# Expert tiles of 128 slots, two to a job, with second weights resident and ys groups summed among the last jobs

## The chip, the cores and the metric

The kernel runs on one core of a Trainium2 chip. The metric is the device time of one execution in microseconds. The engines are TensorE (PE in the rows; PEld is its weight loading), VectorE (DVE), ScalarE (ACT), GpSimd (POOL) and SyncE (SP), which here issues most of the DMA transfers. An engine takes its instructions in their written order; semaphores order the engines among each other.

## The reference

A block with two halves. The first is a layer norm, a scan over time that trains a small MLP (a gradient step for every time step) and its application. The second, the only one that the change touches, is a layer norm and a mixture of experts:

```python
logits = jnp.einsum('btd,ed->bte', x, w_router)
probs = jax.nn.softmax(logits, axis=-1)
vals, idx = jax.lax.top_k(probs, TOP_K)                 # TOP_K = 2 of 8 experts
gates = jnp.sum(jax.nn.one_hot(idx, N_EXPERTS, dtype=x.dtype) * vals[..., None], axis=-2)
hs = jax.nn.gelu(jnp.einsum('btd,fd->btf', x, Ws1) + bs1)   # shared expert
acc = jnp.einsum('btf,df->btd', hs, Ws2) + bs2
h = jax.nn.gelu(jnp.einsum('btd,efd->btef', x, W1) + b1)
y = jnp.einsum('btef,edf->bted', h, W2) + b2
acc = acc + jnp.einsum('bted,bte->btd', y, gates)
return SCALE * acc
```

There are 4 x 1024 tokens of 128 features, the hidden width is 512, all is float32. Only the two chosen experts of a token are computed.

## The kernel before

Up to about 352 us the program does the first half. Then 4096 tokens in 8 groups (NG) of 4 chunks of 128 are normalised and routed. Every token is written twice into the DRAM buffer xs by GpSimd (dispatch, an indirect transfer of 128 rows): each expert has a region there, and the slots in it are filled in the order of the tokens.

The work behind that is a list of jobs, JOBS. An expert job takes a tile of 256 consecutive slots of one expert (39 tiles, since the fill of each expert is known only at run time: 8192 slots and a partly filled tile for each expert). A shared job takes 256 tokens through the shared expert; nine of its 16 tiles are done before the list begins, five stand between the first expert tiles and two at the end. The first N_FULL = 9 tiles are full ones from the first half of the tokens, so they can run while GpSimd still dispatches the second half.

Which expert and which rows a tile has is computed on VectorE into the tables e_i and row_i (full_tiles for the first nine, other_tiles for the rest, the latter between post(6) and post(7) ahead of the list). For each tile SyncE reads these with value_load and issues two transfers: rows(j), 256 rows of xs into xt, and weights(j), the expert's two weight matrices and biases into slab, a ring of RW = 5 buffers. weights(j) waits until VectorE has added tile j-5's bias (e_yb), rows(j) until tile j-4 has been turned (e_tx). The program order of SyncE is: weights of the first five tiles, then for each tile rows(j), weights(j); weights of tiles 9 and 10 come ahead of the rows of tile 9, which need the end of the dispatch.

On TensorE a loop over the list does this for job i:

```python
for i in range(len(JOBS)):
    feed_for(i + 2)
    if i + 1 < len(JOBS):
        e_up(i + 1)
    e_down(i)
```

feed turns the rows of a tile (two 128x128 transposes), VectorE copies them to hg (e_high), e_up makes four 128x256 products with the first weights, ScalarE applies the gelu (e_gelu, one activation for each product), and e_down makes eight 128x128 products with the second weights. VectorE adds the bias and scales the rows with their gates (e_post); its order for job i is prepare(i + 2), which is e_high and meta, then e_post(i). GpSimd scatters the 256 result rows to ys in DRAM, at twice the token's index plus 0 or 1 (scatter, two indirect transfers a tile); rows that belong to no token of this expert go to dump rows.

When all scatters have landed (all_scattered), SyncE loads ys in eight groups into yg, TensorE adds the two results of each token with two products by the identity, VectorE multiplies by the gate, adds to xr, and SyncE and ScalarE store the groups to the output. In the trace a float32 product shows as two MATMUL instructions with two weight loads.

## Time and profile before

| | us |
|---|---|
| median of 3 runs (lowest, highest) | 633.46 (633.27, 637.78) |
| the profiled execution, its own time | 635.85 |
| its span, first to last instruction | 634.1 |
| TensorE matmuls busy | 576.8 (91%) |
| VectorE busy | 427.3 (67%) |
| GpSimd busy | 389.8 (61%) |
| ScalarE busy | 333.7 (53%) |

The span is what the trace covers; the execution's own time is 1.75 us longer. Times of the trace count from the first instruction. Busy time of TensorE is that of overlapping, pipelined instructions; how long a piece of work really takes is read from the starts of consecutive ones.

### The profile page before, as it was taken

The numbers are of one execution on the slowest core, as the hardware profiler recorded it, in microseconds if no ns is written. First come the engines' busy times: TensorE is split into PE (matmuls) and PEld (weight loads), VectorE is DVE, ScalarE is ACT, GpSimd is POOL, SyncE is SP. The second block draws the span as 40 slices with busy tenths as digits, with TensorE's granted clock in tenths as the row PEclk, the third lists the DMA queues.
The fourth block names the chain that finished last, engine by engine and source line by source line (L and its number), as shares of the span: only waits on it lengthen the run. The fifth ranks groups of instructions, "written<-read, shape, count | busy, mean of one in ns | idle before, by whom it ended". The sixth has DMA issues, their size and how long they took to land. (4 is left out here: it accounts for less than half of the span.)

```text
span 634.1 us, 14457 instructions
## 1 busy us (share of the span) xinstructions
PE 576.8 (91%) x4324; PEld 512.9 (81%) x4324; DVE 427.3 (67%) x1730; ACT 333.7 (53%) x1064; POOL 389.8 (61%) x598
## 2 busy tenths in 40 slices
PE   2469999999999999999996967899999999999976
PEld 2249999899999999999984566788999999999952
DVE  3736888788788888878885579876553455545426
ACT  2455666566666656666662374894444444444410
POOL 1526666656666665666662607888888888887520
PEclk9999999999999999999998869899999999999989
DMA  9069930000000000000000001163564778777357
GB/s 196 6 260 394 395 150 1 2 0 0 0 0 0 0 0 0 0 0 0 2 2 1 2 0 39 45 231 95 156 186 130 216 244 247 230 235 232 103 201 212
DMA packets 39797, 66.77 MB, mean 105 GB/s; under 512 B 7523, under 2 KB 26725, under 8 KB 39749
## 3 DMA queue, kind: packets, MB, share of 16 engines
q1 hardware_dynamic: 31076, 54.85, 27.5%
q0 software_dynamic: 4544, 9.45, 4.2%
q10 hardware_dynamic: 4128, 1.91, 1.4%
q8 instruction: 22, 0.36, 0.2%
q14 instruction: 27, 0.21, 0.1%
HBM read 36.26 MB, written 29.92 MB: 104 GB/s over the span
## 5 line engine op out<-in xcount | busy, mean ns | idle before, releaser
L1575 ACT ACTIVATE hid<-bank,slab 128x256 f32<-128x256 f32 x156 | 64.2, 471 | 80.6 <-PE bank L1428 80.5
L1987 POOL DMA_INDIRECT ys<-yo,dst x78 | 75.2, 964 | 28.9 <-issue 16.6
L1979 POOL DMA_INDIRECT xs<-hrow,slot_i x64 | 62.7, 979 | 35.4 <-issue 35.4
L1442 PEld LDWEIGHTS bank<-slab,hid 128*128 128x128 f32 x624 | 75.8, 192 | 2.0
L1442 PE MATMUL bank<-slab,hid 128*128 128x128 f32 x624 | 76.0, 275 | 0.0
L1428 PE MATMUL bank<-hg,slab 128*128 128x256 f32 x312 | 73.7, 380 | 0.4 <-DVE hg L1842 0.4
L1875 DVE TENSOR_TENSOR yb<-bank,slab 128x256 f32<-128x256 f32 x39 | 16.6, 425 | 74.1 <-PE bank L1442 74.1
L1428 PEld LDWEIGHTS bank<-hg,slab 128*128 128x128 f32 x312 | 56.3, 190 | 6.7 <-issue 0.6
L986 POOL TENSOR_TENSOR nL<-aL,ones 128x128 f32<-128x128 bf16 x32 | 16.9, 528 | 41.4 <-ACT aL L695 41.4
L409 PE MATMUL bank<-aH,W2p 128*128 128x128 f32 x192 | 42.1, 301 | 0.1
L409 PE MATMUL bank<-kv,W1b 128*128 128x128 f32 x192 | 41.4, 298 | 0.0
L998 POOL TENSOR_TENSOR nH<-aH,ones 128x128 f32<-128x128 f32 x32 | 14.6, 457 | 36.7 <-ACT aH L713 36.7
L1962 POOL MEMSET rested<- 128x1408 f32 x25 | 32.3, 1291 | 0.0
L409 PEld LDWEIGHTS bank<-aH,W2p 128*128 128x128 f32 x192 | 28.9, 190 | 3.3 <-DVE W2p L790 0.3
L409 PE MATMUL bank<-GX,ge 128*128 128x128 f32 x128 | 30.7, 322 | 0.6 <-DVE ge L790 0.5
L409 PEld LDWEIGHTS bank<-kv,W1b 128*128 128x128 f32 x192 | 29.8, 196 | 0.1
L990 POOL TENSOR_TENSOR oL<-tL,ones 128x128 f32<-128x128 f32 x32 | 14.6, 456 | 24.7 <-ACT tL L698 24.7
L1880 DVE TENSOR_SCALAR yo<-yb,gt 128x128 f32<-128x128 f32 x78 | 26.5, 471 | 1.4
L1013 POOL TENSOR_TENSOR diff<-ge 128x256 f32<-128x256 f32 x32 | 23.3, 728 | 5.5 <-DVE sums L793 5.5
L790 DVE SCALAR_TENSOR_TENSOR gL<-qrowL,bank 128x128 bf16<-128x128 bf16 x64 | 18.4, 287 | 11.1 <-ACT qrowL L706 5.5
L970 POOL TENSOR_TENSOR GXb<-GX,ones 128x256 bf16<-128x256 f32 x32 | 23.3, 729 | 4.0 <-DVE GX L790 2.1
L409 PE MATMUL bank<-hT,wkv 128*128 (+1 forms) x128 | 23.3, 307 | 2.5 <-POOL arowL L1033 2.5
(340 smaller groups left out, 1872.3 us busy)
## 6 DMA issues: line engine op xcount, KB each, us to landing
slab<-in_slabs_dram SPq DMA_DIRECT2D x39, 578.0 KB, 4.2
xs<-fill SPq DMA_DIRECT2D x34, 528.0 KB
xt<-xs SPq DMA_DIRECT2D x39, 132.0 KB
yg<-ys SPq DMA_DIRECT2D x8, 512.0 KB, 6.7
xr<-in_L_attn_x_dram SPq DMA_DIRECT2D x16, 128.0 KB, 6.9
ys<-yo,dst POOLq DMA_INDIRECT x78, 3.8
xs<-hrow,slot_i POOLq DMA_INDIRECT x64, 2.5
out_dram<-xr SPq DMA_DIRECT2D x16, 64.0 KB, 1.8
```

What stands on the lines that cost most here:

```text
L409: return pe.matmul(dst, lhs, rhs, start=start, stop=stop, skip_group_check=True)
L790: return dve.scalar_tensor_tensor(out=dst, in0=a, scalar=s, in1=b, op0=o0, op1=o1)
L970: pool.tensor_tensor(GXb[r][:, :, :].rearrange("p k t -> p (k t)"), GX[r][:, :, :].rearrange("p k t -> p (k t)"), ones2[:, :], ALU.mult).t ...
L986: pool.tensor_tensor(nL[1][:, :], aL[1][:, :], ones2[:, 0:P], ALU.subtract).then_inc(l_n, 1)
L1013: pool.tensor_tensor(diff[:, :, :], ge[r % 2][1][:, :, :], ge[r % 2][0][:, :, :], ALU.subtract).then_inc(chk_d, 1)
L1428: mm = pe.matmul(e_half(i, n), left[:, n * P:(n + 1) * P], right, start=True, stop=True)
L1442: mm = pe.matmul(y[:, s * D:(s + 1) * D], hid[i % 2][:, n, s * P:(s + 1) * P], right, start=(n == 0), stop=(n == FT - 1), skip_group_check ...
L1575: nc.scalar.activation(hid[i % 2][:, n, :], e_half(i, n), ACT.Gelu_apprx_tanh, bias=bias).then_inc(e_x, 1)
L1880: dve.tensor_scalar(yo[v][:, s, :], yb[i % 2][:, s, :], gt[v][:, s:s + 1], None, ALU.mult).then_inc(e_yo, 1)
L1962: nc.gpsimd.memset(rested[:, :], 0.0).then_inc(pause_done, 1)
L1979: pool.indirect_dma_start(out=xs[:, :], out_offset=bass.IndirectOffsetOnAxis(ap=slot_i[:, i, c:c + 1], axis=0), in_=hrow[:, c, :], in_offs ...
L1987: pool.indirect_dma_start(out=ys[:, :], out_offset=bass.IndirectOffsetOnAxis(ap=dst[v][:, s:s + 1], axis=0), in_=yo[v][:, s, :], in_offset ...
```

## The change

- A tile is 128 slots (HALF), and an expert job takes two of them, which may belong to different experts. There are 72 half tiles, so 36 expert jobs in place of 39; 12 of them (N_FULL) come before the end of the dispatch, in place of 9.
- SyncE reads an expert and a row for each half: two rows transfers of 128 rows and two slab transfers a job. A slab now holds the first weights and the biases only; the ring has RW = 4 buffers of two slabs.
- The second weights of all experts are loaded once into w2 (2 MB). e_down on TensorE reads the experts of its two halves from e_i and picks the weights by register.
- e_up makes eight products of 128 columns; e_gelu eight activations.
- The tiles behind the first twelve are listed in three parts: by the end of the first half, of the third quarter and of all of the dispatch. The tables for them are computed in four pieces on VectorE behind jobs 1 to 4. So after BY_HALF (20) jobs' tiles the first four groups of ys are complete, after BY_THREE (28) two more.
- SyncE loads groups 0 to 3 of ys after the weights of tiles 30 to 33, groups 4 and 5 behind the last tile, 6 and 7 when all scatters have landed. VectorE adds the two results itself for groups 0 to 6 (group_step, three operations a group, among the posts of jobs 34 to 42 and behind them); TensorE does it for group 7.

```diff
-SLAB = 2 * F + FT + D
-N_TILES = (2 * B * S) // TS + E - 1
+SLAB = F + FT + D
+HALF = P
+N_HALVES = -(-((2 * B * S) // HALF + E - 1) // SUB) * SUB
+N_TILES = N_HALVES // SUB
 CAP = B * S
 N_SH = B * S // SH
 PARTS = ((0, 2), (2, 4), (4, 6), (6, 8))
 LONGEST = 8
-N_FULL = -(-(B * S - E * (TS - 1)) // TS)
+N_FULL = -(-(B * S - E * (HALF - 1)) // HALF) // SUB
+FULL = N_FULL * SUB
...
+BY_HALF = -(-((B * S + E * (HALF - 1)) // HALF) * HALF // TS)
+BY_THREE = -(-((3 * B * S // 2 + E * (HALF - 1)) // HALF) * HALF // TS)
...
+LOAD_AT = N_TILES - 6
+ADD_AT = len(JOBS) - (N_SH - EARLY_SH - 5) - 7
 RX = 4
 RY = 10
-RW = 5
+RW = 4
...
-            slab = [psb(f"slab{i}", [P, SLAB]) for i in range(RW)]
+            slab = [psb(f"slab{i}", [P, SUB, SLAB]) for i in range(RW)]
+            w2 = psb("w2", [P, E, F])
             hg = [psb(f"hg{i}", [P, TS]) for i in range(2)]
-            hid = [psb(f"hid{i}", [P, FT, TS]) for i in range(2)]
+            hid = hs
...
-                    e = sp.value_load(e_i[0:1, j:j + 1], min_val=0, max_val=E - 1)
-                    sp.dma_start(slab[j % RW][:, :], slabs[:, bass.ds(e, 1), :].rearrange("p o w -> p (o w)")).then_inc(s_slab[j % RW], 16)
+                    for s in range(SUB):
+                        e = sp.value_load(e_i[0:1, SUB * j + s:SUB * j + s + 1], min_val=0, max_val=E - 1)
+                        sp.dma_start(slab[j % RW][:, s, :], slabs[:, bass.ds(e, 1), :].rearrange("p o w -> p (o w)")).then_inc(s_slab[j % RW], 16)
 
                 def rows(j):
                     if j >= RX:
                         sp.wait_ge(e_tx, j - RX + 1)
                         sp.wait_ge(meta_ready, j - RX + 1)
-                    row = sp.value_load(row_i[0:1, j:j + 1], min_val=0, max_val=XS_ROWS - TS)
-                    sp.dma_start(xt[j % RX][:, :, :], xs[bass.ds(row, TS), :].rearrange("(s p) w -> p s w", p=P)).then_inc(s_xt[j % RX], 16)
-
+                    for s in range(SUB):
+                        row = sp.value_load(row_i[0:1, SUB * j + s:SUB * j + s + 1], min_val=0, max_val=XS_ROWS - HALF)
+                        sp.dma_start(xt[j % RX][:, s, :], xs[bass.ds(row, HALF), :]).then_inc(s_xt[j % RX], 16)
+
+                sp.dma_start(w2[:, :, :], e_w2).then_inc(s_w2, 16)
...
-                all_scattered(sp)
-                for g in range(NG):
-                    load(sp, g)
-                for g in range(0, NG, 2):
-                    store(sp, g)
+                    if j == LOAD_AT:
+                        scattered(sp, BY_HALF)
+                    if LOAD_AT <= j < LOAD_AT + 4:
+                        load(sp, j - LOAD_AT)
+                scattered(sp, BY_THREE)
+                load(sp, 4)
+                load(sp, 5)
+                store(sp, 0)
+                store(sp, 2)
+                scattered(sp, N_TILES)
+                load(sp, 6)
+                load(sp, 7)
+                store(sp, 4)
+                store(sp, 6)
...
-                        mm = pe.matmul(e_half(i, n), left[:, n * P:(n + 1) * P], right, start=True, stop=True)
+                        if kind == "expert":
+                            for s in range(SUB):
+                                mm = pe.matmul(e_half(i, n)[:, s * P:(s + 1) * P], slab[j % RW][:, s, n * P:(n + 1) * P],
+                                               hg[j % 2][:, s * P:(s + 1) * P], start=True, stop=True)
+                        else:
+                            mm = pe.matmul(e_half(i, n), left[:, n * P:(n + 1) * P], right, start=True, stop=True)
...
+                    if kind == "expert":
+                        if j == 0:
+                            pe.wait_ge(s_w2, 16)
+                            pe.wait_ge(table_ready, 2)
+                        if j == N_FULL:
+                            pe.wait_ge(table_ready, 4)
+                        expert = [pe.value_load(e_i[0:1, SUB * j + s:SUB * j + s + 1], min_val=0, max_val=E - 1) for s in range(SUB)]
                     if i >= 2:
                         pe.wait_ge(e_yb, i - 1)
                     for s in range(SUB):
                         for n in range(FT):
                             if s == 0:
                                 pe.wait_ge(e_x, FT * i + n + 1)
-                            right = slab[j % RW][:, F + n * P:F + (n + 1) * P] if kind == "expert" else sw[:, 1, n, :]
+                            right = w2[:, bass.ds(expert[s], 1), n * P:(n + 1) * P].rearrange("p o w -> p (o w)") if kind == "expert" else sw[:, 1, n, :]
...
-                for g in range(NG):
-                    pe.wait_ge(s_yg[g], 16)
-                    if g >= 2:
-                        pe.wait_ge(sum_used, g - 1)
-                    for k in range(2):
-                        mm = pe.matmul(bank[6 + g % 2][:, :], ident[:, :], yg[g][:, :, k * D:(k + 1) * D], start=(k == 0), stop=(k == 1))
-                    mm.then_inc(sum_ready, 1)
+                pe.wait_ge(s_yg[NG - 1], 16)
+                for k in range(2):
+                    mm = pe.matmul(bank[7][:, :], ident[:, :], yg[NG - 1][:, :, k * D:(k + 1) * D], start=(k == 0), stop=(k == 1))
+                mm.then_inc(sum_ready, 1)
...
+                        if kind == "expert":
+                            nc.scalar.activation(hid[i % 2][:, n, 0:P], e_half(i, n)[:, 0:P], ACT.Gelu_apprx_tanh,
+                                                 bias=slab[j % RW][:, 0, F + n:F + n + 1])
+                            nc.scalar.activation(hid[i % 2][:, n, P:TS], e_half(i, n)[:, P:TS], ACT.Gelu_apprx_tanh,
+                                                 bias=slab[j % RW][:, 1, F + n:F + n + 1]).then_inc(e_x, 1)
...
+                def rest_marks():
+                    grid = [P, V, CAP // HALF]
+                    dve.wait_ge(turned, NG)
+                    then(dve.tensor_tensor(over_all, held[:, :, :].rearrange("p k e -> p (k e)").unsqueeze(2).broadcast_to(grid),
+                                           cut["step"].unsqueeze(1).broadcast_to(grid), ALU.is_gt))
+                    then(dve.tensor_reduce(marks[:, E:4 * E], over_all, AX_X, ALU.add))
...
+                def rest_ends():
+                    then(dve.tensor_tensor(number[:, :], marks[:, E:4 * E], marks[:, 0:3 * E], ALU.subtract))
...
+                    for k in range(3):
+                        then(dve.tensor_tensor(tri[:, k * E:(k + 1) * E, :], number[:, k * E:(k + 1) * E].unsqueeze(1).broadcast_to([P, E, E]),
+                                               cut["tri"].rearrange("p (a b) -> p a b", b=E), ALU.mult))
+                    then(dve.tensor_reduce(last[:, :, :].rearrange("p k e -> p (k e)"), tri[:, :, :], AX_X, ALU.add))
+                    for k in range(1, 3):
+                        then(dve.tensor_scalar(last[:, k, :], last[:, k, :], last[:, k - 1, E - 1:E], None, ALU.add))
+
+                def rest_experts():
+                    then(dve.tensor_tensor(later, cut["tile"][:, 0:n_rest].unsqueeze(2).broadcast_to([P, n_rest, V]),
+                                           last[:, :, :].rearrange("p k e -> p (k e)").unsqueeze(1).broadcast_to([P, n_rest, V]), ALU.is_ge))
+                    then(dve.tensor_reduce(etab[:, rest], later, AX_X, ALU.add))
+                    for k in range(1, 3):
+                        then(dve.scalar_tensor_tensor(out=etab[:, rest], in0=later[:, :, k * E - 1], scalar=-float(E), in1=etab[:, rest],
+                                                      op0=ALU.mult, op1=ALU.add))
+                    dve.tensor_scalar(e_i[:, rest], etab[:, rest], float(E - 1), None, ALU.min).then_inc(table_ready, 1)
+
+                def rest_rows():
...
+                    then(dve.tensor_tensor(later, later, weight[:, :].unsqueeze(1).broadcast_to([P, n_rest, V]), ALU.mult))
+                    then(dve.tensor_reduce(first[:, rest], later, AX_X, ALU.add))
...
+                    dve.tensor_copy(row_i[:, rest], rowf[:, rest]).then_inc(table_ready, 1)
+
+                def group_step(k):
+                    g = k // 3
+                    y, xc = ysum[g % 2][:, :, :], xr[:, g * GRP:(g + 1) * GRP, :]
+                    if k % 3 == 0:
+                        dve.wait_ge(s_yg[g], 16)
+                        dve.tensor_tensor(y, yg[g][:, :, 0:D], yg[g][:, :, D:2 * D], ALU.add).then_inc(sum_used, 1)
+                    elif k % 3 == 1:
+                        dve.wait_ge(sum_used, 2 * g + 1)
+                        dve.tensor_tensor(y, y, gate[:, 1, :].unsqueeze(1).broadcast_to([P, GRP, D]), ALU.mult).then_inc(sum_used, 1)
+                    else:
+                        dve.wait_ge(sum_used, 2 * g + 2)
+                        dve.wait_ge(sh_ready, min(N_SH, (g + 1) * GRP // SUB))
+                        dve.tensor_tensor(xc, y, xc, ALU.add).then_inc(fin_ready, 1)
...
+                    if i == 1:
+                        rest_marks()
+                    elif i == 2:
+                        rest_ends()
+                    elif i == 3:
+                        rest_experts()
+                    elif i == 4:
+                        rest_rows()
+                    elif ADD_AT <= i < ADD_AT + 4:
+                        group_step(2 * (i - ADD_AT))
+                        group_step(2 * (i - ADD_AT) + 1)
+                    elif ADD_AT + 4 <= i < ADD_AT + 7:
+                        group_step(i - ADD_AT + 4)
+                        if i == ADD_AT + 6:
+                            group_step(11)
+                            group_step(12)
+                    elif i == ADD_AT + 7:
+                        group_step(13)
+                for k in range(14, 18):
+                    group_step(k)
```

How this stands in the instruction streams. SyncE, before: one tile of the steady state, its rows and the next weights. ISA rows are register operations and the check of the value's bounds.

```order
L1295 TENSOR_LOAD row_i [waits h_e,h_W1]
L1295 ISA x2
L1296 ISA
L1296 DMA xt0<-xs 128x2x132
L1288 TENSOR_LOAD e_i [waits h_T2]
L1288 ISA x2
L1289 ISA
L1289 DMA slab3<-in_slabs_dram 128x1156
```

SyncE now, at the same place: the two rows transfers of a tile and the first of its two slab transfers.

```order
L1306 TENSOR_LOAD row_i [waits h_e,h_W1]
L1306 ISA x2
L1307 ISA
L1307 DMA xt0<-xs 128x132
L1306 TENSOR_LOAD row_i
L1306 ISA x2
L1307 ISA
L1307 DMA xt0<-xs 128x132
L1298 TENSOR_LOAD e_i [waits h_T2]
L1298 ISA x2
L1299 ISA
L1299 DMA slab0<-in_slabs_dram 128x644
```

A tile has four groups of a table read, register operations and an issue, in place of two; only the first of each pair carries waits.

TensorE, before: e_up of a tile (L1428) and e_down of the one before it (L1442).

```order
L1428 MATMUL bank2<-hg0,slab0 128x256 [waits h_Tq,h_U2,h_n]
L1428 MATMUL bank2<-hg0,slab0 128x256
L1428 MATMUL bank3<-hg0,slab0 128x256 x2
L1442 MATMUL bank4<-slab4,hid0 128x128 [waits h_Tq,h_T2]
L1442 MATMUL bank4<-slab4,hid0 128x128 [waits h_Tq] x3
L1442 MATMUL bank4<-slab4,hid0 128x128 x4
```

TensorE now: the last products of e_up (L1450), then the start of e_down (L1466, L1474).

```order
L1450 MATMUL bank2<-hg0,slab2 128x128 x3
L1450 MATMUL bank3<-hg0,slab2 128x128 x4
L1466 TENSOR_LOAD e_i
L1466 ISA x2
L1466 TENSOR_LOAD e_i
L1466 ISA x2
L1474 ISA [waits h_Tq,h_T2]
L1474 MATMUL bank4<-w2,hs0 128x128
L1474 ISA [waits h_Tq]
L1474 MATMUL bank4<-w2,hs0 128x128
L1474 ISA [waits h_Tq]
```

Two table reads stand ahead of the first down product, and a register operation, which carries the wait for the gelu, ahead of each.

VectorE now, behind the post of job 3 (rest_experts) and up to the copy of the next tile's columns (L1907); before, nothing stood between a post and that copy.

```order
L1868 TENSOR_SCALAR last<-last 128x8 [waits et_step] x2
L1939 TENSOR_TENSOR yb1<-bank5,slab2 128x256 [waits h_Ta,et_step]
L1944 TENSOR_SCALAR yo2<-yb1,gt2 128x128 [waits h_e,h_T2]
L1944 TENSOR_SCALAR yo2<-yb1,gt2 128x128
L1871 TENSOR_TENSOR xn<-tabs,last 128x1152
L1873 TENSOR_REDUCE etab<-xn 128x48 [waits et_step]
L1875 SCALAR_TENSOR_TENSOR etab<-xn,etab 128x48 [waits et_step] x2
L1877 TENSOR_SCALAR e_i<-etab 128x48 [waits et_step]
L1907 COPY hg0<-bank6 128x256 [waits h_U1,h_W1]
L1913 TENSOR_TENSOR other<-xt0,etab 128x2
```

These operations have moved from ahead of the list into it.

## Rows read from the trace of the kernel before

**Rows 1.** Windows by stage, core 0: busy time (instructions) of each engine, clock, DMA

```profile
438.00:490.00 52.00, 51.19 (x347) 47.83 (x348) 24.27 (x86) 23.08 (x56) 42.81 (x43) 1.00 0.51 147
490.00:598.00 108.00, 108.00 (x754) 102.02 (x753) 55.18 (x231) 47.65 (x116) 84.90 (x83) 1.00 0.74 224
```

**Rows 2.** The chain of waits from 430 to 500: start, duration, what

```profile
482.80 2.24 DMA xt<-xs
...
485.53 1.73 PE bank L1428 x8
487.26 1.78 PE bank L1442 x16
```

**Rows 3.** Timeline of TensorE, 438 to 484: start, us, instructions merged

```profile
439.24 3.69 PE L1428 MATMUL bank<-hg,slab 128*128 128x256 f32 x16 [0.39 <-DVE hg L1842]
...
455.52 0.38 PE L1410 MATMUL bank<-ident,xt 128*128 128x128 f32 x2
...
459.26 0.38 PE L1410 MATMUL bank<-ident,xt 128*128 128x128 f32 x2
...
481.21 1.89 PE L1428 MATMUL bank<-hg,slab 128*128 128x256 f32 x8
```

**Rows 4.** Timeline of SyncE's transfer issues, 426 to 634

```profile
433.43 8.57 SPq L1296 DMA_DIRECT2D xt<-xs  x6
...
486.36 0.34 SPq L1289 DMA_DIRECT2D slab<-in_slabs_dram  x1
487.53 0.37 SPq L1296 DMA_DIRECT2D xt<-xs  x1
...
491.01 0.35 SPq L1289 DMA_DIRECT2D slab<-in_slabs_dram  x1
```

**Rows 5.** The instructions of line 1288 on SyncE: ns min/median/max

```profile
L1288 SPq TENSOR_LOAD <-e_i x39: 262/273/448, 415.0 to 586.6; - x39
L1288 SPq FUSED_REGOPS  x39: 147/147/154, 415.3 to 586.9; - x39
L1288 SPq SEQ_ASSERT  x39: 18/18/18, 415.5 to 587.1; - x39
```

**Rows 6.** The page's list of transfers: KB each, us from issue to landing

```profile
slab<-in_slabs_dram SPq DMA_DIRECT2D x39, 578.0 KB, 4.2
...
xt<-xs SPq DMA_DIRECT2D x39, 132.0 KB
```

**Rows 7.** Timelines of all engines and of VectorE: start, us, instruction, idle before

```profile
432.32 0.40 DVE L1798 TENSOR_REDUCE etab<-past 128x30 f32<-128x240 f32 x1
...
434.47 0.24 DVE L1807 TENSOR_SCALAR rowf<-rowf,taken 128x30 f32<-128x30 f32 x1
...
478.54 0.42 DVE L1842 COPY hg<-bank 128x256 f32<-128x256 f32 x1
...
616.12 0.69 DVE L1947 TENSOR_TENSOR ysum<-bank,gate 128x512 f32<-128x512 f32 x1 [5.61 <-PE bank L1520]
```

**Rows 8.** The chain of waits from 598, then a row of TensorE's timeline

```profile
602.50 1.80 PE bank L1442 x16
...
605.83 0.96 POOL ys L1987
...
607.09 2.24 DMA ys<-yo,dst
...
609.47 3.81 DMA yg<-ys
...
613.33 15.71 PE bank L1520 x32
...
629.79 0.69 DVE xr L1951
...
614.96 0.34 PEld L1520 LDWEIGHTS bank<-yg,ident 128*128 128x128 f32 x1 [0.47 <-DMA yg<-ys]
```

158 lines of the change are left out of this document (75 added, 83 removed).

## The prediction

> **What bounds the kernel now.** The change touches only the last third of the program, so I read the profile in this order. The windows by stage show what TensorE does there: it is busy for 51.19 of 52 us between 438 and 490, and for all of 108 us between 490 and 598, at full granted clock [rows 1]. VectorE, ScalarE and GpSimd are busy for 51%, 44% and 79% of the second window. The chain of waits agrees: from 485.53 it is nothing but TensorE's up and down matmuls, 1.73 and 1.78 us a job [rows 2]. The timeline of TensorE gives the pitch: 455.52 to 459.26, 3.74 us for an expert job (0.22 of them for turning a tile's rows), 3.51 for a shared one [rows 2, 3]. Behind the jobs comes a tail in one chain: the last expert matmul ends at 604.30, the last rows of ys have landed at 609.33, the first group of them is back at 613.28, TensorE sums eight groups for 15.71 us, VectorE ends at 630.48 and the output at 634.1 [rows 8]. So 46 jobs bound 165 us, then 30 us are a serial tail.
>
> The engine to look at next is SyncE. It reads each tile's expert and row from a table before it can issue the transfer. With all waits over, four such steps take 486.36 to 491.01, 1.16 us each, with two more issues between the rows shown [rows 4]; in a step the table read is 0.27 us, its register operations 0.15, the issue itself 0.35 [rows 4, 5]. Two steps a tile, 2.3 us, now hide under 3.74.
>
> **The change part by part.** Times below are in the trace of before, whose span is 634.1.
>
> Fewer jobs. Tiles go from 39 to 36, jobs from 46 to 43. Tensor work of an expert job: the four up products on 256 columns become eight on 128, 16 instructions in place of 8. The down product already has that shape, 16 instructions in 1.78 us [rows 2], so up costs 1.78 in place of 1.73, and a loop is 3.78. Taken by TensorE alone: 3 x 3.74 saved, 36 x 0.05 lost, 9.4 us gained.
>
> SyncE. Each tile now needs two rows transfers and two slab transfers, four steps of 1.16, which is 4.64 us, more than TensorE's 3.78. Halving the bytes does not halve a step: slab transfers of 578 KB and rows transfers of 132 KB are both issued at that pitch [rows 4, 6]. The bounds for a step are 1.0 (if the second of a pair, which has no waits, saved all that lies between the shown parts) and 1.2; I take 1.16. Where five shared jobs lie between the first twelve tiles this is covered. For the 24 tiles behind them nothing covers it, and SyncE becomes what the jobs wait for.
>
> TensorE's own table reads. The second weights are resident, so e_down reads two experts into registers and computes an address before each of eight products. By SyncE's rows a read with its checks is 0.27 + 0.15 + 0.02 [rows 5], up to 0.8 with the gaps, so 0.9 to 1.6 us a job, and up to 0.15 for each of the eight address operations. Whether this costs anything depends on how far TensorE's instruction stream runs ahead of its array, which this trace doesn't show. What it must be ahead by is worked out so: the address operations wait for the gelu results. A gelu of 128 columns costs less than 0.47 us and the eight overlap, so they end some 3.8 us after the job's up began, against 5.5 us for the start of its down. The stream has 1.7 us of lead there, and between two such points it must fit the reads into 3.78. I take it as hidden (cost 0), with 1.6 us a job as the other end. The Trainium skill's page "TensorE: Matmul & The Clock Gate" (section on the array's architecture) gives TensorE an instruction queue 64 deep, which would hold most of a job's 72 weight loads and matmuls, and speaks for hiding; no run here shows it. The page "DMA: Bandwidth & Descriptors" (Latency and other measured facts) puts the floor of a table read at about 600 ns; the trace has 273 ns, and by the page's figure, an estimate, a SyncE step would be 1.5 us and the 24 tiles' stage 31 us longer.
>
> VectorE. The tables of the later tiles move from ahead of the jobs (they were hidden there: TensorE was still at work) into jobs 1 to 4, and grow. An operation on 240 elements takes 0.40 and on 512 0.69 [rows 7], 1.07 ns an element, so 768 elements take 0.97 and 1152 take 1.37; small ones 0.24. rest_marks is 2 x 0.97 = 2.0, rest_ends about 2.2, rest_experts 2 x 1.37 + 3 small = 3.4, rest_rows 2 x 1.37 + 4 small = 3.8. Between the copy of hg (ends 478.96) and the up that reads it (481.21) there are 2.25 us [rows 3, 7]. Playing the four jobs through with VectorE's own 1.8 us a job, the copies for jobs 6 and 7 come 0.9 and 2.1 us late: 3.0 us lost, bounds 0 and 5. Later, 18 summing operations of 0.69, two a job, fit into the slack of 4.64 us jobs.
>
> The tail. Four groups of ys are loaded during the last tiles, two more behind them, and VectorE adds six (and then the seventh) itself. After the last ys rows have landed only two loads, one sum on TensorE and one group on VectorE are left, in place of 8 loads and 32 matmuls.
>
> ScalarE does eight gelus in place of four; it is at 44% [rows 1] and stays under 80% of a loop. GpSimd issues 72 scatters in place of 78 at an unchanged pitch; it was not late at 598 and has more time a tile now. The DMA engines carry 12% more bytes per tile (slabs of 660 KB in place of 578) but fewer tiles, over longer jobs. These cost 0.
>
> **The sum.** Rows transfers start at 433.43 [rows 4]. The fourth of them (tile 1's second half) starts 3 x 1.16 later and lands in 2.24 [rows 2]: up(0) begins at 439.4 (439.24 before [rows 3]). To the end of down of job 13 TensorE has 15 ups, 14 downs and 10 turns: 11 x 1.78 + 4 x 1.73 + 14 x 1.78 + 10 x 0.22 = 53.6, so 493.0, with VectorE's delay 496.0. Job 13 is tile 9; when VectorE has added its bias (0.45 later, 496.45) its slab buffer is free, and since SyncE waits there in order ahead of tile 12's rows, everything else starts from this point. Up to the last rows transfer, that of tile 35, SyncE has 2 + 48 + 42 = 92 steps: 106.7 us; four loads of yg at 0.5 are put among them: 605.2. The rows land at 607.0. Then 0.22 for the turn and three more loops (down of tile 35 comes two jobs after its turn): 10.6, at 617.9, against 602.5 to 604.3 for tile 38's in the old kernel. From there to the landed ys rows 5.03 as before [rows 8]: 622.9. Two loads: the first took 3.81, the second of before was there by 614.96, 5.5 after [rows 8]; with only two in flight I take 4.9 and 0.1 for the issue: 627.95. TensorE's sum to VectorE's start 2.79 (613.33 to 616.12 [rows 7, 8]), two operations 1.42, output 3.62: 635.8.
>
> That is a span 1.7 us longer: the tail falls from 29.8 us after the last expert matmul to 17.9, and this and the three jobs pay for SyncE's pace. The profiled execution took 635.85 us for its span of 634.1, and 637.5 would be the same for the new kernel; the median of the runs lies 2.4 lower, at 633.46, so I predict 635.2. About 1% (6 us) is what a measurement of this kernel can tell from no change.
>
> **Rivals.** (A) The forecast: SyncE paces the later tiles, 629 to 642 with the bounds of step, VectorE's delay and loads. A hundredth of a us in the step is 0.9 us in the end. Chance 0.53, mostly within 1%, with its upper edge beyond.
>
> (B) Slower: TensorE's table reads are not hidden. At 1.6 us a job a loop is 5.4. Twelve tiles of the first stage add 19 us, and the 24 others, bounded by TensorE now and not by SyncE, 24 x 0.74 = 18: 672. It begins to cost in the first stage as soon as the instruction stream needs over 3.78 us a job (at 4.3, 6 us in all: 641), and everywhere over 4.64. For it speaks that the address operations carry the waits, so the stream stops at each gelu; against it the 1.7 us of lead. Chance 0.25.
>
> (C) Faster: SyncE doesn't bind, because steps without waits overlap better than the rows of before show. It decides at 0.95 us a step; then TensorE paces all jobs, down of tile 35 ends at about 601 in place of 617.9 and the time is 618. Against it: the pitch of 1.16 holds wherever steps follow each other. Chance 0.12.
>
> (D) The change doesn't do what it says at the tail: VectorE stands in front of a group that hasn't landed, with the jobs' posts behind it, or the last loads are held up. Up to half of the 12 us gained there goes: 641. The first load is issued some 9 us ahead of its use, which speaks against it. Chance 0.10.
>
> **How the numbers follow.** Faster by over 1%: C and a corner of A, 0.15. Slower by over 1%: B, half of D and the upper edge of A, 0.38. The rest 0.47. For eight in ten the range reaches up into B and down to half of the way to C: 624 to 658.
>
> **What would show it.** In the new trace SyncE's steps should follow without a pause from about 497 to 605 at 4.64 a tile, TensorE should idle 0.8 us a tile on rows just landed, and be without a pause in the first stage but for jobs 5 and 6, where VectorE's copy is late. Idle time ahead of the down products, put down to nothing or to TensorE's own sequencer, would be B. A tile pitch of 3.8 late in the program would be C. I would be wrong in size if reading SyncE's table slows down while TensorE reads it too.

## The result and the profile after

The changed kernel took 651.8 us (median of 4 runs, 647.6 to 656.8). The kernel before, on the same chip at the same time, took 635.6 (4 runs, 633.3 to 640.3). The ratio is 1.023, with an interval of 1.017 to 1.029: slower by 2.3%. The forecast was 635.2 with a range of 624 to 658, so the time lies in the range, and on the side that had a chance of 0.38, 16.6 us above the forecast itself. The profiled execution has a span of 650.0 us against 634.1, at a mean granted clock of 0.961 against 0.976.

The windows by stage of the changed kernel (columns as in [rows 1]):

```profile
438.00:500.00 62.00, 56.07 (x429) 53.91 (x428) 37.37 (x121) 28.00 (x93) 51.43 (x49) 0.94 0.53 150
500.00:560.00 60.00, 53.68 (x453) 52.20 (x453) 23.35 (x114) 29.64 (x108) 37.26 (x37) 0.97 0.64 186
560.00:630.00 70.00, 59.82 (x505) 57.57 (x505) 33.27 (x136) 32.04 (x116) 38.53 (x38) 1.00 0.77 229
```

TensorE, which was busy in 159 of 160 us of this part before [rows 1], is now busy in 169.6 of 192, and its clock is below full in the first two windows. What it waits for is in the view of waits (443 to 629 us: engine, line, releaser, us in total, times, longest):

```profile
PE bank L1431 <- DMA xt<-xs: 16.4, 13, 3.5
PE bank L1450 <- issue: 4.8, 2, 3.3
```

16.4 us go to rows that have not landed when a tile's turn comes (L1431), 4.8 us to two waits ahead of up products (L1450). Those two are where VectorE has tables to build. TensorE's timeline (start, us, instructions merged, idle before and its end), to be laid beside [rows 3]:

```profile
443.91 3.81 PE L1450 MATMUL bank<-hg,slab 128*128 128x128 f32 x32 [0.39 <-DVE hg L1907]
...
466.08 2.02 PE L1450 MATMUL bank<-hg,slab 128*128 128x128 f32 x16 [1.53 <-issue]
467.94 1.95 PE L1474 MATMUL bank<-sw,hs 128*128 128x128 f32 x16
473.18 3.76 PE L1450 MATMUL bank<-hg,slab 128*128 128x128 f32 x16 [3.29 <-issue]
476.73 3.19 PE L1474 MATMUL bank<-w,hs 128*128 x16
479.75 0.38 PE L1431 MATMUL bank<-ident,xt 128*128 128x128 f32 x2
...
505.95 1.95 PE L1450 MATMUL bank<-hg,slab 128*128 128x128 f32 x16
507.74 1.95 PE L1474 MATMUL bank<-w,hs 128*128 x16
513.17 0.47 PE L1431 MATMUL bank<-ident,xt 128*128 128x128 f32 x2 [3.48 <-DMA xt<-xs]
513.45 3.58 PE L1453 MATMUL bank<-hT,sw 128*128 128x256 f32 x8
```

And VectorE at the second of the two waits, with the GpSimd operation beside it (two timelines, the second a single row):

```profile
467.50 1.34 DVE L1880 TENSOR_TENSOR xn<-xn,weight 128x1152 f32<-128x1152 f32 x1
468.88 1.35 DVE L1881 TENSOR_REDUCE first<-xn 128x48 f32<-128x1152 f32 x1
470.26 0.21 DVE L1882 TENSOR_TENSOR rowf<-tabs,first 128x48 f32<-128x48 f32 x1
470.51 1.78 DVE L1883 TENSOR_SCALAR rowf<-rowf,marks 128x48 f32<-128x48 f32 x1
472.32 0.21 DVE L1884 SCALAR_TENSOR_TENSOR rowf<-etab,rowf 128x48 f32<-128x48 f32 x1
472.56 0.19 DVE L1887 CAST row_i<-rowf 128x48 int32<-128x48 f32 x1
472.66 0.42 DVE L1907 COPY hg<-bank 128x256 f32<-128x256 f32 x1
```

```profile
470.96 1.27 POOL L2055 TENSOR_TENSOR xr<-xr,gsb 128x512 f32<-128x512 f32 x1
```

The copy of hg, for which the up at 473.18 waits, stands in order behind rest_rows. rest_rows takes 5.16 us (467.50 to 472.66), of which 1.78 is an operation on 48 elements that takes 0.2 elsewhere in the same list; it ends when GpSimd's operation does (472.29 and 472.23). When TensorE comes back, its next 16 products take 3.76 us and then 3.19 in place of 1.95. The granted clock is 0.91 from 470 to 473 us, 0.50 (the lower of its two levels) from 473 to 476.5, 0.60 from there to 480 and 1.00 again behind it. The same happens at 513.45, where eight products take 3.58 in place of 1.89 (granted clock 0.57 from 513 to 517).

From there on SyncE sets the pace. Its timeline of issues, in the steady part and at its end (compare [rows 4]):

```profile
516.71 1.43 SPq L1299 DMA_DIRECT2D slab<-in_slabs_dram  x2
518.96 1.42 SPq L1307 DMA_DIRECT2D xt<-xs  x2
521.14 1.43 SPq L1299 DMA_DIRECT2D slab<-in_slabs_dram  x2
523.40 1.42 SPq L1307 DMA_DIRECT2D xt<-xs  x2
...
612.34 1.46 SPq L1299 DMA_DIRECT2D slab<-in_slabs_dram  x2
614.62 1.42 SPq L1307 DMA_DIRECT2D xt<-xs  x2
```

Pair follows pair at 2.2 us, 4.43 us for the four steps of a tile (516.71 to 521.14), where TensorE needs 3.78. Over thirteen tiles (527.67 to 586.68) the mean is 4.54, since single steps take a few tenths longer now and then. The end, in the chain of waits (compare [rows 8]; the last expert product ends at 628.96):

```profile
630.67 0.96 POOL ys L2074
631.62 0.30 POOLq L1200
631.93 3.47 DMA ys<-yo,dst
635.72 0.34 SPq L1278
636.11 5.09 DMA yg<-ys
641.24 3.79 PE bank L1549 x4
645.06 0.70 DVE ysum L2034
645.78 0.69 DVE xr L2038
```

21.0 us from the last expert product to the end, where it was 29.8.

### The profile page after: what moved, and what is told of

Its sections match the earlier page's. It is cut to its first block and busy times, and to the rows that moved or that the text cites. A ratio compares the mean times of both kernels' runs of the same rounds, so it can differ in the third digit from the quotient of the medians.

```text
span 650.0 us, 15857 instructions
## 1 busy us (share of the span) xinstructions
PE 567.3 (87%) x4506; PEld 513.9 (79%) x4506; DVE 436.8 (67%) x1755; ACT 347.8 (54%) x1196; POOL 383.9 (59%) x591
## 3 DMA queue, kind: packets, MB, share of 16 engines
q10 hardware_dynamic: 4128, 1.91, 1.3%
## 5 line engine op out<-in xcount | busy, mean ns | idle before, releaser
L2074 POOL DMA_INDIRECT ys<-yo,dst x72 | 69.5, 966 | 58.1 <-DVE yo L1944 46.0
L1604 ACT ACTIVATE hs<-bank,slab 128x128 f32<-128x128 f32 x144 | 54.9, 381 | 83.5 <-PE bank L1450 83.5
L2066 POOL DMA_INDIRECT xs<-hrow,slot_i x64 | 64.3, 1004 | 35.5 <-issue 35.2
L1450 PE MATMUL bank<-hg,slab 128*128 128x128 f32 x576 | 72.0, 280 | 5.2 <-issue 4.8
L1450 PEld LDWEIGHTS bank<-hg,slab 128*128 128x128 f32 x576 | 68.7, 196 | 5.8 <-issue 5.8
L1474 PE MATMUL bank<-w,hs 128*128 x576 | 71.5, 278 | 0.0
L1474 PEld LDWEIGHTS bank<-w,hs 128*128 128x128 f32 x576 | 69.2, 195 | 0.5
L1939 DVE TENSOR_TENSOR yb<-bank,slab 128x256 f32<-128x256 f32 x36 | 15.3, 424 | 76.8 <-PE bank L1474 76.8
L1606 ACT ACTIVATE hs<-bank,slab 128x128 f32<-128x128 f32 x144 | 55.5, 386 | 0.0
L2049 POOL MEMSET rested<- 128x1408 f32 x24 | 30.9, 1289 | 0.0
L416 PEld LDWEIGHTS bank<-kv,W1b 128*128 128x128 f32 x192 | 29.8, 196 | 0.1
L1431 PE MATMUL bank<-ident,xt 128*128 128x128 f32 x72 | 14.5, 285 | 17.2 <-DMA xt<-xs 16.4
```

Of the source, the lines that this page charges most:

```text
L416: return pe.matmul(dst, lhs, rhs, start=start, stop=stop, skip_group_check=True)
L1431: tr = pe.transpose(fed(j)[:, s * P:(s + 1) * P], xt[j % RX][:, s, 0:D], ident[:, :])
L1450: mm = pe.matmul(e_half(i, n)[:, s * P:(s + 1) * P], slab[j % RW][:, s, n * P:(n + 1) * P], hg[j % 2][:, s * P:(s + 1) * P], start=True, s ...
L1474: mm = pe.matmul(y[:, s * D:(s + 1) * D], hid[i % 2][:, n, s * P:(s + 1) * P], right, start=(n == 0), stop=(n == FT - 1), skip_group_check ...
L1604: nc.scalar.activation(hid[i % 2][:, n, 0:P], e_half(i, n)[:, 0:P], ACT.Gelu_apprx_tanh, bias=slab[j % RW][:, 0, F + n:F + n + 1])
L1606: nc.scalar.activation(hid[i % 2][:, n, P:TS], e_half(i, n)[:, P:TS], ACT.Gelu_apprx_tanh, bias=slab[j % RW][:, 1, F + n:F + n + 1]).then_ ...
```

## The experiments

They are numbered e1 to e12 in the order below (e1 is the first, with one more table read). They ran in three groups of four, each group on one chip with the kernel before beside it. Which chip the result came from is not on record; its time for the kernel before (635.6) and its trace are like those of the first group. The kernel before took 634.4 us on the first chip, 642.8 on the second, 643.3 on the third, so only ratios are compared between groups. A second figure is used where a profiled run began its jobs early or late: the time from up(0), the first product of the job list, to the end of the span. It is 206.1 us in the changed kernel (443.91 to 650.0). Three theories were on trial. SyncE: its four steps a tile pace the jobs behind the dispatch. VectorE: the tables hold up the first jobs. TensorE's table reads (the rival B): they cost time ahead of each down product.

**One more table read in each slab step.** On SyncE, in weights:

```diff
                     for s in range(SUB):
                         e = sp.value_load(e_i[0:1, SUB * j + s:SUB * j + s + 1], min_val=0, max_val=E - 1)
+                        e = sp.value_load(e_i[0:1, SUB * j + s:SUB * j + s + 1], min_val=0, max_val=E - 1)
```

> The changed kernel, but SyncE reads the expert of each half tile twice: two more table reads with their checks for a tile, by the trace 0.27 + 0.15 + 0.02 us each, about 0.5 with gaps. If SyncE paces the 24 tiles behind the dispatch, the time grows by 24 x 1.0 us = 24 (to some 675 against 651.8), since every step of its stream counts. If TensorE's own table reads pace the jobs, SyncE has 0.3 us a tile to spare and more, and the time grows by 17 or less; if TensorE's matmuls paced them (3.78 a loop against 4.43 for SyncE now, 5.4 then) the growth would be 24 as well, but from a lower level that the trace of the changed kernel excludes.

Measured: ratio 1.055 (1.047 to 1.064), 673.2 us, span 670.1. That is 3.2 points more than the changed kernel, 20 us for 48 more reads with their register operations behind the dispatch. This profiled run began its jobs at 439.15 us, 4.8 earlier than the changed kernel's; from up(0) on it takes 231.0 us in place of 206.1, 24.9 more, as the expectation has it. That is 0.52 for each read, where one alone is 0.27 + 0.15 and gaps [rows 5]. A step on SyncE is on the path with its full price.

**No table reads on TensorE.** The second weights of fixed experts are used, so that e_down reads no table and computes no address; the rows of the expert tiles are then other numbers than the reference's, with the same work.

```diff
-                        expert = [pe.value_load(e_i[0:1, SUB * j + s:SUB * j + s + 1], min_val=0, max_val=E - 1) for s in range(SUB)]
+                        expert = [(SUB * j + s) % E for s in range(SUB)]
```

> The changed kernel without the table reads and address operations on TensorE: the second weights are those of a fixed expert (the results of the expert tiles are not the reference's). If TensorE's stream runs far enough ahead, as the trace of the changed kernel suggests (no idle time ahead of the down products outside jobs 4 to 6), nothing changes: 652 within 5. If the reads cost their 0.9 to 1.6 us a job, 30 to 50 us go.

Measured: 650.2 us, ratio 1.018 (1.008 to 1.027), and a span of 650.0, to the tenth that of the changed kernel. Rival B is out. The changed kernel's trace shows what was hidden (line 1466, TensorE's sequencer, ns min/median/max):

```profile
L1466 PEldq TENSOR_LOAD <-e_i x72: 296/301/710, 445.7 to 625.2; - x72
L1466 PEldq FUSED_REGOPS  x72: 146/151/156, 446.1 to 625.7; - x72
```

0.45 us a read, 0.9 a job, and no idle time of TensorE before a down product (L1474) in that trace.

**Shorter steps on SyncE.** One table read brings both values of a pair, and the check of their bounds is left out (the table's values keep them):

```diff
-                    for s in range(SUB):
-                        e = sp.value_load(e_i[0:1, SUB * j + s:SUB * j + s + 1], min_val=0, max_val=E - 1)
+                    _, both = nc.values_load_multi_w_load_instructions(
+                        e_i[0:1, SUB * j:SUB * (j + 1)], engines=[mybir.EngineType.SP], min_val=0, max_val=E - 1, ...)
+                    for s in range(SUB):
+                        e = both[s]
```

and the same for the rows.

> The changed kernel with cheaper SyncE steps: one table read fetches both values of a pair, and the bounds checks are left out (the tables are clamped). By the durations in the trace a tile's four steps, 4.43 us now, lose 2 x 0.35 for reads and 4 x 0.2 for checks: 2.9 us, below TensorE's 3.78. If SyncE paces the late tiles, 24 x 0.65 = 16 us go: 636. If it does not, nothing goes.

Measured: 636.4 us, ratio 1.001 (0.996 to 1.006), span 631.8. SyncE's timeline in that kernel:

```profile
544.25 0.85 SPq L1302 DMA_DIRECT2D slab<-in_slabs_dram  x2
545.85 0.85 SPq L1313 DMA_DIRECT2D xt<-xs  x2
547.95 0.89 SPq L1302 DMA_DIRECT2D slab<-in_slabs_dram  x2
```

Pair follows pair at 1.6 us (544.25 to 545.85) in place of 2.2, so SyncE now waits for the others: a tile takes 3.79 us on average (521.54 to 567.05, twelve tiles), which is TensorE's own pace. TensorE's waits for rows fall from 16.4 to 7.0 us. The ratio gives back all 2.3 points, but not all of that is SyncE: in the profiled run the jobs also began at 439.19 in place of 443.91 us. From up(0) to the end it takes 192.6 us, 13.5 less than the changed kernel. With the first experiment, this shows SyncE's pace from both sides. Reading both values at once and leaving out the bounds check were not tried apart.

**Tables spread over nine jobs.** The four functions are cut in nine and one piece is put behind each of jobs 1 to 9.

```diff
-                    if i == 1:
-                        rest_marks()
-                    elif i == 2:
-                        rest_ends()
-                    elif i == 3:
-                        rest_experts()
-                    elif i == 4:
-                        rest_rows()
+                    if 1 <= i < 10:
+                        (rest_marks, rest_counts, rest_ends, rest_experts, rest_sums,
+                         rest_names, rest_rows, rest_firsts, rest_last)[i - 1]()
```

> The changed kernel with the tables of the late tiles computed in nine pieces behind jobs 1 to 9, none over 2.2 us, in place of four behind jobs 1 to 4. In the trace the pieces of 4.0 and 5.1 us made the copies of hg late and TensorE waited 1.5 and 3.3 us, then ran at the lower clock: 8.4 us in all against plain matmul time. If VectorE's tables are the cause, the time falls by 7 to 8 us, to 644. If the stall came from TensorE's table reads, which first occur at the same jobs, nothing changes.

Measured: 645.3 us, ratio 1.012 (1.003 to 1.021), span 644.1. Its waits (442 to 623 us):

```profile
PE bank L1431 <- DMA xt<-xs: 17.3, 12, 3.6
PE bank L1450 <- issue: 1.1, 1, 1.1
```

The waits ahead of up products fall from 4.8 to 1.1 us, the waits for rows stay. So VectorE's tables cost about 6 us (the medians are 6.5 apart, the times from up(0) 4.9, and the intervals of the two ratios overlap): they push out the release from which SyncE's chain starts, and behind it nothing is won back.

**The sums at the end, as before.** All eight groups are loaded behind the jobs and summed by TensorE.

```diff
-                    if j == LOAD_AT:
-                        scattered(sp, BY_HALF)
-                    if LOAD_AT <= j < LOAD_AT + 4:
-                        load(sp, j - LOAD_AT)
...
+                scattered(sp, N_TILES)
+                for g in range(NG):
+                    load(sp, g)
```

> The changed kernel with the old tail: all eight groups of ys loaded behind the last scatter and summed by TensorE. From the end of the last expert matmul to the end of the span the old kernel took 29.8 us and the changed one 21.0. If the early sums are what shortens the tail, and cost nothing among the jobs, the time grows by 8.8 us, to 661 (1.037 of the kernel before). If the early loads hold up SyncE (4 loads at 0.5 us) and VectorE, part of that comes back: 657.

Measured: 678.3 us, ratio 1.055 (1.050 to 1.060), nearly two points above the forecast. The next three were above theirs too, by 1.6, 0.8 and 1.1 points. The changed kernel itself, run again below on another chip of the slower kind, has 1.039 there, and against that the late sums cost 1.6 points, 10 us, as the expectation has it. The trace has 31.5 us from the last expert product to the end (644.59 to 676.1), against 20.8 for the changed kernel run again.

**SyncE's queue in another order.**

```diff
-                weights(N_FULL)
-                weights(N_FULL + 1)
                 sp.wait_ge(s_half[1], 16 * CH)
                 for j in range(N_FULL, N_TILES):
                     rows(j)
-                    if j >= N_FULL + 2:
-                        weights(j)
+                    weights(j)
```

> The changed kernel with SyncE's order changed at the border of the two stages: the rows of tile 12 come ahead of its weights, so that only the weights wait for the slab buffers of tiles 8 and 9, and the rows of tiles 12 and 13 are on their way before. Behind the point where tile 9's slab comes free SyncE then has four steps (4.4 us) less, and TensorE's stall of 3.5 us there, with the lower clock behind it, goes. If SyncE's chain from that point sets the end, 4 to 6 us go: 647. If it does not, the stall alone goes and is given back later: 652.

Measured: 664.1 us, ratio 1.034 (1.029 to 1.039), above both forecasts. It is read again with the control below.

**Tiles of 256 slots, with the rest of the change.** Slabs, rows transfers and products as before, 39 tiles; the three lists with their tables in jobs 1 to 4 and the early sums stay. In SyncE's part:

```diff
-                    for s in range(SUB):
-                        row = sp.value_load(row_i[0:1, SUB * j + s:SUB * j + s + 1], min_val=0, max_val=XS_ROWS - HALF)
-                        sp.dma_start(xt[j % RX][:, s, :], xs[bass.ds(row, HALF), :]).then_inc(s_xt[j % RX], 16)
+                    row = sp.value_load(row_i[0:1, j:j + 1], min_val=0, max_val=XS_ROWS - TS)
+                    sp.dma_start(xt[j % RX][:, :, :], xs[bass.ds(row, TS), :].rearrange("(s p) w -> p s w", p=P)).then_inc(s_xt[j % RX], 16)
```

> Only the second part of the change: tiles of 256 slots as in the kernel before (39, one expert and one slab each, second weights in the slab, two SyncE steps a tile, no table reads on TensorE), but with the three lists, their tables behind jobs 1 to 4, and the early sums. If the half tiles cost what SyncE's steps say, this has the shorter tail (9 to 11 us) without them; the tables are smaller (30 tiles in place of 48) and cost 1 to 5 us. So 624 to 630, faster than both kernels. If the loss lies in the lists or the early sums, it is at 645 or above.

Measured: 640.5 us, ratio 0.994 (0.991 to 0.998): faster than the kernel before, by less than expected, and 4.5 points under the 1.039 of the control. TensorE waits twice in the first jobs (3.45 and 2.17 us), and then, but for 0.2 us, not again until the last job. Behind the wait of 3.45 us its clock did not fall: the granted clock stays at 1.00, and eight products of 256 columns take 1.97 us where they take 1.89 without a wait.

```profile
471.23 1.97 PE L1445 MATMUL bank<-hg,slab 128*128 128x256 f32 x8 [3.45 <-issue]
```

**Short steps, the other order and spread tables together.**

> The changed kernel with the three mendings together: short SyncE steps, rows ahead of weights at the border, and the tables in nine pieces. Alone, the first took 14 us and the third 7; the second should take 5 but overlaps with the first, since short steps already catch up. If they add, 626 to 631 (TensorE paces all jobs: three jobs fewer than before and the shorter tail, 20 us at most below the kernel before, less what 128 column products and stalls cost). If some other wait takes their place, 634 or more.

Measured: 643.1 us, ratio 1.000 (0.997 to 1.004): above the forecast, in the part of the expectation in which some other wait takes their place. Jobs began only at 453.13 us in the profiled run. Four ratios above their forecasts on one chip are the reason for the next run.

**The changed kernel once more.**

> The kernel of the change, not altered, beside the three that follow, on the same chip. Its first ratio to the kernel before was 1.023 (1.017 to 1.029). The theory that the last four experiments missed because of their edits says 1.023 again, on any chip (651 us where the kernel before takes 636, 658 where it takes 643). The rival says that on the chip of those four, where the kernel before itself took 1.3% longer, SyncE's reads and the fetching of instructions are slower for every kernel of this form: there it says 1.03 or more, a SyncE pitch of 4.7 us or more a tile instead of 4.43, and short waits of TensorE put down to 'issue' in the middle of a group of products.

Measured: 668.9 us, ratio 1.039 (1.034 to 1.044), span 664.0. What the rival foretold is there: a ratio over 1.03, short waits inside groups of products, and a SyncE pitch of 4.93 us a tile on average (534.72 to 598.83, thirteen tiles) where the first trace has 4.54. The same program is 1.6 points worse against the kernel before on this chip than on the first. Its jobs began as before (443.66 us); the whole difference lies behind that, 220.3 us from up(0) on in place of 206.1. Its trace has waits in the middle of a group of products, which are not there in the first trace (TensorE's timeline):

```profile
504.12 1.06 PE L1474 MATMUL bank<-w,hs 128*128 x8
505.48 0.37 PE L1474 MATMUL bank<-w,hs 128*128 x1 [0.30 <-issue]
506.89 0.95 PE L1474 MATMUL bank<-w,hs 128*128 x7 [1.04 <-issue]
```

and on SyncE, instructions that do next to nothing and take 0.7 us now and then. First the changed kernel on its first chip, then here (line 1298, ns min/median/max):

```profile
L1298 SPq TENSOR_LOAD <-e_i x72: 262/268/398, 422.1 to 617.2; - x72
L1298 SPq SEQ_ASSERT  x72: 18/18/18, 422.7 to 617.7; - x72
```

```profile
L1298 SPq TENSOR_LOAD <-e_i x72: 3/268/721, 415.0 to 630.6; - x72
L1298 SPq SEQ_ASSERT  x72: 3/18/726, 415.6 to 631.1; - x72
```

The medians are the same, so a step is not slower in itself as a rule. Single instructions are stretched, and between steps there are pauses in which no instruction of that queue runs. What it pauses for, the trace does not show. That each engine's instructions arrive late is my guess; it was not isolated. The same sign separates all the traces: the MOVE ahead of a slab's issue, 29 ns in the median of the changed kernel, takes up to 0.45 to 0.73 us in those of e5 to e12 and at most 0.04 in the first trace and in those of e1 to e4.

**Short steps and spread tables,** without the other order.

> Both mends together, without the other order of the queue: one table read on SyncE for the two values of a pair, and the tables of the rest in nine pieces behind jobs 1 to 9. The theory (SyncE's steps pace the jobs behind the dispatch, and VectorE's tables hold the first jobs) says that they add: 1.023 less 2.2 points for the short steps, less 1.1 points for the spread tables, 0.990 of the kernel before, about 629 us on a chip where that takes 635.6, since with short steps SyncE has slack and can no longer take back what the spread tables give. The rival, that short steps alone had won by luck of an early start of the jobs (438.2 against 442.9 us), says 1.00 to 1.01.

Measured: 646.5 us, ratio 1.005 (1.001 to 1.009). Against the changed kernel beside it, 3.3% less: the sum of the two single gains on the first chip, 2.2 and 1.1. They add, and neither takes the other's. My forecast of 0.990 started from 1.023; from 1.039 the same sum gives 1.006. The measured ratio also lies where the rival had it (1.00 to 1.01), but the rival counted from 1.023 too, and its own reason is absent here: the jobs began at 442.76 us, only 0.9 earlier than in the changed kernel beside it, and from up(0) on the kernel took 199.5 us in place of 220.3. What keeps it from being faster than the kernel before, with three jobs fewer and the shorter tail, was not isolated; its trace still has 17 us of waits of TensorE among the jobs, 7.3 of them for rows and 7.1 ahead of up products.

**Tiles of 256 slots with spread tables.**

> Tiles of 256 slots as before, with the three lists and the sums among the last jobs, and the tables in nine pieces. The theory says: 0.994 measured with the tables behind four jobs; its trace shows 3.45 and 2.17 us of waiting in the first jobs and about 2 us at half the clock behind them, all given back: 0.982 to 0.986, 624 to 627 us on a chip where the kernel before takes 635.6. The rival, that the waits of the first jobs come from collisions of VectorE with GpSimd and merely move to other jobs, says 0.992 to 0.996.

Measured: 636.7 us, ratio 0.989 (0.982 to 0.995), the best of all kernels here, 1.1% faster than the kernel before and 4.8% faster than the changed one. The interval takes in both theories' figures. Its trace, 443 to 628 us:

```profile
PE bank L1534 <- DMA yg<-ys: 6.2, 1, 6.2
PE bank L1427 <- issue: 3.9, 1, 3.9
PE bank L1445 <- issue: 2.3, 3, 1.6
```

The waits ahead of up products (L1445) have gone from 6.3 us in four waits to 2.3 in three. The expectation read about 2 us at half the clock into the trace of the kernel without spread tables; as said there, that trace does not have them. The 3.9 us stand at the turn (L1427) of the first tile behind the dispatch, whose rows are issued at 488.47.

**The other order once more.**

> The same kernel as in e6 (SyncE waits for the dispatch ahead of the first slab of the rest, then takes each tile's rows ahead of its slabs), now beside the kernel of the change on the same chip. If the order itself costs nothing, its time is that of the kernel of the change within 0.5%, or up to 1% below it for the wait of 3.5 us at tile 12 that it takes away; e6 was then slow because of its chip. If the order costs (the slabs of tiles 12 and 13 can no longer be fetched while SyncE waits for the dispatch, four steps of 1.11 us that then stand in the paced chain: 4.4 us), it is 0.5 to 1% above the kernel of the change beside it.

Measured: 665.6 us (663.6 to 669.1), the changed kernel beside it 668.9 (665.8 to 671.7); ratio to the kernel before 1.034 (1.029 to 1.039). The wait of 3.7 us at tile 12 is gone from TensorE's timeline and some 0.5% with it, less than the two intervals can tell from nothing. By the order of the queue four slab steps now stand in the paced chain in place of being issued during the wait; that they took back the rest is argued and not shown. e6 had the same 1.034 on the second chip, so I read e5 to e8 as points against 1.039. That the second chip and the third are alike rests on this one pair of times, and on the pauses, which the traces of both chips have.

## Why the prediction came out as it did

The mechanism that the forecast was built on held: SyncE's four steps a tile pace the jobs behind the dispatch. What was mis-sized most is the sum's term for VectorE's delay in jobs 1 to 4, with the start of the jobs and the tail off in the same direction. That the time lies in the range is in part luck: the upper end of the range, 658, was there for rival B, which did not happen, and the forecast's own range ended at 642. Against my own timeline of span 635.8, the 14.2 us more are the four terms below, and 0.3 us by which job 13's bias was added later than I had it (506.7, 0.8 behind the end of its down and not 0.45).

**Start of the jobs, +4.5.** up(0) at 443.91, not 439.4. Of this 0.9 was there at 351, ahead of the first line that the change touches. The rest came in the routing stage. There VectorE's operations are stretched to 1.5 to 2.5 us where they run beside a GpSimd operation, as at 387.66 us, where 64 elements took 1.52 us and their neighbours 0.22:

```profile
387.40 0.23 DVE L1750 SCALAR_TENSOR_TENSOR zs<-bank,top 128x64 f32<-128x64 f32 x1
387.66 1.52 DVE L1753 SCALAR_TENSOR_TENSOR wide<-zs,tabs 128x64 f32<-128x64 f32 x1
```

```profile
387.80 1.29 POOL L2055 TENSOR_TENSOR xr<-xr,gsb 128x512 f32<-128x512 f32 x1
```

Between 350 us and up(0), eight single VectorE operations of the changed kernel's trace take over 1.4 us, and four of the kernel before. In the traces of the first group there are two kinds: e2 and e4 have nine and eight, at nearly the same places, and begin at 443.98 and 442.87; e1 and e3 have four and five and begin at 439.15 and 439.19, as early as the kernel before (439.24), though they load w2 and compute the same tables. So I take this term as the way the two engines happened to stand in a run and no price of the change. That is argued from the traces; no run tested it by itself, and on the other chips the two do not go together so well (e9 has four such operations and begins at 443.66, e12 eight and 448.81, e8 nine and 453.13).

**First stage, +5.4.** From up(0) to the end of job 13's down it took 62.0 us, where I had 53.6 and VectorE's 3.0. Two copies were late, those for jobs 6 and 7 as predicted, by 1.53 and 3.29 us in place of 0.9 and 2.1. rest_experts and rest_rows took 3.99 and 5.16 us, not 3.4 and 3.8, most of the excess from the one operation beside GpSimd's. The other 3.0 us I had not thought of at all: after the second wait 32 products ran at the lower clock (473.18 to 479.75 is 6.57 us, 3.57 at the full one). The three make 7.8 us, and with some tenths spread over the other jobs it is 8.4 in place of 3.0, above the upper bound of 5. The spread tables (e4) gave about 6 us back, which agrees.

**SyncE, +0.9.** The release of tile 9's slab came at 506.7 and the last expert product ended at 628.96, 122.3 us behind it; I had 121.45. The step was 1.11 us, not 1.16, and the tile 4.43, not 4.64, which is 4.6 us less over 92 steps. It went back into a pause of 2.1 us at 525 to 527 us, where SyncE waited for VectorE to release a slab behind the slowed products of 513.45; into the four loads of yg, which cost 2.6 us in the queue and not 2.0; into single steps that took 0.3 to 0.5 us longer, some 2 us; and into the last rows, which were turned 2.4 us behind their issue and not 1.8. The sign that I had named, 0.8 us of idle time of TensorE a tile, came as 12.9 us for 24 tiles (the 16.4 less the 3.5 at 513.17), 0.54 a tile and in clumps. The pace is shown by the trace, its price by e1, e3 and e10. That the table reads hide on TensorE is shown by e2.

**Tail, +3.1.** 21.0 us, not 17.9. The last rows of ys had landed 6.4 us behind the last expert product and not 5.0 (635.40), the loads took 5.5 us from there on and the issue 0.3, and from TensorE's sum to VectorE's start it was 3.8 (2.79 in my sum), again below full clock: the granted clock is 0.50 from 641 us to the end. Nothing in the record says why the last transfers took longer than before. The 8.8 us that the early sums save against before are borne out by e5, which loses 10 without them, though the two kernels compared there ran on two chips.

The sum's last line took 2.4 us off, since the median of three runs of before lay below its profiled execution; with the fourth run the two are 0.2 apart (635.62 and 635.85). The profiled execution of the changed kernel is at its median (651.81 and 651.8), so that line was wrong too. Rival A, the forecast, is the mechanism; its range of 629 to 642 was too narrow because it moved each term by itself and gave the clock no term. The slower result came from beyond its upper edge, and not from B. B and C are refuted (B by e2, C by the pitch of 4.43), and D, half of 12 us lost, came true by 3.1 us through other causes than the ones it named.

## What to carry to other kernels

Halving the unit of work doubles the steps of the engine that issues its transfers, and a step with an address read from a table has a price that does not fall with the bytes (1.1 us here). Compare steps a job times that price with the job before cutting tiles, and read both values of a pair at once if it doesn't fit. Work that moves into a pipeline stands in line ahead of the small copies on which the bounding engine waits: cut it to less than the slack of one job (2.25 us here), and reckon behind a wait of about 3 us of TensorE with the lower clock as well, which cost up to 3.0 us more here, 1.4 in e2, and nothing in e7. And a verdict within 2% needs the control on the same chip; here one program stood at 1.023 on one chip and at 1.039 on another.

## What the runs showed of the hardware

- A table read with its register operations costs TensorE's queue 0.30 and 0.15 us, and two of them and eight computed addresses a job cost its array nothing (span 650.0 with and without). The Trainium skill's page "TensorE: Matmul & The Clock Gate" (section on the array's architecture) has an instruction queue of 64 ahead of the array; the run agrees in that such reads are hidden.
- VectorE operations on 8 to 64 elements took 1.5 to 2 us in place of 0.2 when a GpSimd tensor operation of 1.27 us ran beside them, and ended with it or less than 0.1 us after. The records begin at 470.51 (VectorE) and 470.96 (GpSimd), so an operation of 0.2 us that began first was held all the same. A longer one, 512 elements at 399.64, took 2.48 in place of 0.69 and ended 0.6 us after GpSimd's. The Trainium skill's page "GPSIMD Engine Reference" (Specifications) says that GpSimd shares its SBUF interfaces with VectorE and names contention with instructions of a 2-port mode or with two SBUF inputs. The traces agree in kind, and show that such a small VectorE operation stood until the other ended. Other operations beside GpSimd's were not stretched.
- TensorE's clock fell to the lower level after waits of 3.29 and 3.48 us in the midst of full work, and 16 products took up to 3.76 us in place of 1.95. After the wait of 1.53 us it did not. The length of the wait alone does not decide it: in e7 the clock stayed after 3.45 us, and in e4 it fell after 1.91 us (559.82), where 16 products then took 3.52 us. How long it stays low differs too: behind the same wait of 3.29 us, two groups of products took 6.6 us in the changed kernel and 5.0 in e2.
- Instruction queues can pause without a wait that the profile shows, up to 1 us at a time. The eight traces of the second and third chip have such pauses, the five of the changed kernel and of e1 to e4 do not. The same program had a span of 650.0 us without them and 664.0 with them, where the kernel before went from 635.6 to 643.3 in the median. That the chip is the cause is read from three chips and no more.
